# Keys by tokens through GpSimd, a transposing DMA and ScalarE instead of TensorE

## The reference

```python
Q = phi((xn @ Wq + bq)); K = phi((xn @ Wk + bk)); V = xn @ Wv + bv     # phi(z) = elu(z) + 1
def step(carry, qkv):                       # over the tokens
    KV = KV + einsum('bhd,bhe->bhde', ki, vi);  Ks = Ks + ki
    out = (qi . KV) / (qi . Ks + EPS)
y = x + out @ Wo + bo + tree(xn)
```

## Time and profile before

| | us |
|---|---|
| median of 3 runs | 1342.34 |
| lowest, highest | 1339.39, 1344.98 |
| the profiled execution | 1346.16 |
| its span in the profile | 1344.4 |

### The profile page before, as it was taken

The page is one execution under the profiler, slowest core; times in us unless marked ns, Lnnn a source line. Parts: engine busy times, 40 slices in busy tenths (PEclk is TensorE's granted clock), DMA queues, the critical chain, the costliest instruction groups (busy, mean ns, idle before and its releaser), DMA issues.

```text
span 1344.4 us, 49015 instructions
## 1 busy us (share of the span) xinstructions
PE 1266.5 (94%) x22173; PEld 1115.1 (83%) x22173; DVE 844.0 (63%) x2186; ACT 622.1 (46%) x1007; POOL 373.8 (28%) x590
## 2 busy tenths in 40 slices
PE   5899999999989999999999999999999999999987
PEld 4789788888978888888888888889788887887977
DVE  4775766657576574765757566574766757666463
ACT  3553544435445253553536445353553535545351
POOL 3424132141421413223141411413223141321410
PEclk9899999999999999999999999999999999999999
DMA  6000001000000000001000000100001000000000
GB/s 211 18 3 18 18 3 33 3 33 3 10 26 2 33 3 10 26 2 33 2 19 18 10 26 2 34 3 10 26 3 33 3 17 18 2 18 3 17 2 18
DMA packets 21599, 25.95 MB, mean 19 GB/s; under 512 B 1025, under 2 KB 19728, under 8 KB 21392
## 3 DMA queue, kind: packets, MB, share of 16 engines
q1 hardware_dynamic: 21392, 22.82, 5.2%
HBM read 14.43 MB, written 8.39 MB: 17 GB/s over the span
## 4 chain that ended last, share of the span: by engine, by line
PE 78%; DVE 11%; ACT 6%; issue 4%; DMA 1%; SPq 0%; DVEq 0%
PE w_pair L646 16%; PE s_pair L646 16%; PE o_pair L658 8%; PE s_pair L658 8%; PE kv_pair L727 5%; PE o_pair L752 5%; PE o_pair L766 5%; PE s_pair L716 4%; DVE xn L506 3%; PE w_pair L693 3%; PE w_pair L698 3%; ACT ex L407 3%; PE w_pair L680 3%; ACT ex L410 3%; DVE v_aug L529 2%
## 5 line engine op out<-in xcount | busy, mean ns | idle before, releaser
L329 POOL TENSOR_SCALAR_AFFINE_SELECT aT<-aT 64x512 f32<-64x512 f32 x256 | 167.6, 655 | 896.3 <-ACT aT L434 888.0
L646 PE MATMUL w_pair<-xnT,wk 128*128 128x512 f32 x768 | 209.5, 409 | 6.2 <-issue 3.6
L646 PE MATMUL s_pair<-xnT,wq 128*128 128x512 f32 x756 | 195.3, 394 | 0.2 <-issue 0.2
L434 ACT ACTIVATE aT<-s_pair 128x512 f32<-128x512 f32 x128 | 76.5, 597 | 251.6 <-PE s_pair L716 251.6
L577 DVE TENSOR_TENSOR snaps<-kv_pair,snaps 128x65 f32<-128x65 f32 x768 | 173.4, 226 | 26.4
L520 DVE SCALAR_TENSOR_TENSOR kT<-w_pair,bias_one,ex 128x512 f32<-128x512 f32 x128 | 95.9, 749 | 142.4 <-ACT ex L410 142.4
L646 PEld LDWEIGHTS s_pair<-xnT,wq 128*128 128x128 f32 x756 | 143.3, 190 | 32.0 <-issue 0.4
L646 PE MATMUL s_pair<-wv,xnT 128*128 128x512 f32 x648 | 168.6, 395 | 0.0
L646 PEld LDWEIGHTS w_pair<-xnT,wk 128*128 128x128 f32 x768 | 138.4, 192 | 33.1 <-issue 4.4
L410 ACT ACTIVATE ex<-ex 128x512 f32<-128x512 f32 x256 | 161.8, 632 | 8.1
L407 ACT ACTIVATE ex<-w_pair,neg_bias 128x512 f32<-128x512 f32 x130 | 89.4, 688 | 158.1 <-PE w_pair L646 158.1
(11 more groups left out here) (105 smaller groups left out, 2021.6 us busy)
## 6 DMA issues: line engine op xcount, KB each, us to landing
x_in<-in_L_attn_x_dram SPq DMA_DIRECT2D x16, 512.0 KB, 3.8
out_dram<-y_buf SPq DMA_DIRECT2D x32, 256.0 KB, 2.1
stage<-in_L_attn_Wv_dram SPq DMA_DIRECT2D x2, 512.0 KB, 8.1
stage<-in_L_attn_Wk_dram SPq DMA_DIRECT2D x2, 512.0 KB, 9.7
stage<-in_L_attn_Wq_dram SPq DMA_DIRECT2D x2, 512.0 KB, 10.8
stage<-in_L_attn_Wo_dram SPq DMA_DIRECT2D x2, 512.0 KB, 9.1
bv_all<-in_L_attn_bv_dram SPq DMA_DIRECT2D x1, 512.0 KB, 8.7
ffn_tok<-in_L_ffn_Wq_dram SPq DMA_DIRECT2D x1, 256.0 KB
```

Source lines behind the costliest of these rows:

```text
L329: pool.affine_select(out=part, in_=part, compare_op=ALU.is_ge, fill=0.0, base=0, pattern=[[0, 2 * CH], [1, D]], channel_multiplier=-1).the ...
L646: last = pe.matmul(dst, l, r, start=i == 0, stop=i == len(steps) - 1)
```

## The change

The first two units keep the old way. For every unit m from 2 on the keys by tokens are made without TensorE:

- GpSimd's `take_apart(m)` reads kT as 16-bit halves and lays the low halves of all 512 tokens in one plane and the high halves in another (k_planes). It waits until VectorE has made the keys, and until the DMA has read the planes of the unit before.
- SP's `turn_keys(m)` issues one transposing DMA, 128 x 1024 16-bit numbers, from k_planes to k_turned. It waits for GpSimd and until ScalarE is through with k_turned of unit m - 1.
- ScalarE's `put_together(m)` copies k_turned to k_tok and interleaves the halves again, one instruction of 128 x 1024 16-bit numbers. It stands behind the exponential of the queries.

So the fill "kT" leaves the list of a unit. The keys are now computed three units ahead, one more than before, and the queries stay two ahead. "oT" stands last before the "y" fills. TensorE waits for the new k_tok in the midst of the "oT" transposes. Some waits of TensorE are moved or split, `residual` goes from p = 0 to p = 1, the load of x from p = 0 to p = 2, and the stores of a block behind its last unit, on SP's queue. At p = 2 and p = 6 VectorE takes the value fills ahead of queries and output.

```diff
@@ unit_fills
-    ahead = divmod(n + 2, PAIRS) if n + 2 < blocks * PAIRS else None
+    keys = divmod(n + 3, PAIRS) if n + 3 < blocks * PAIRS else None
+    queries = divmod(n + 2, PAIRS) if n + 2 < blocks * PAIRS else None
...
+    fills.append((("oT", p, g), W1))
     if p == PAIRS - 1:
-        fills += [(("oT", p, g), W1), (("y", 0, g), O1)]
-    if ahead:
-        fills.append((("kT", ahead[1], ahead[0]), W0))
-    fills.append((("y", 1, g), S1) if p == PAIRS - 1 else (("oT", p, g), W1))
+        fills += [(("y", 0, g), O1), (("y", 1, g), S1)]
@@ FIRST
-         (("kT", 1, 0), W0)]
+         (("kT", 1, 0), W0), (("K", 2, 0), W0)]
@@ SP
+            def turn_keys(m):
+                sp.wait_ge(k_apart, m - 1)
+                if m > 2:
+                    sp.wait_ge(k_whole, m - 2)
+                sp.dma_start_transpose(k_turned[:, :, :], k_planes[:, :, :].rearrange("p s t -> p (s t)"))\
+                  .then_inc(k_turned_in, 16)
...
+            turn_keys(2)
+            for n in range(UNITS):
+                g, p = divmod(n, PAIRS)
+                if p == 0 and g:
+                    store(g - 1)
+                if n + 3 < UNITS:
+                    turn_keys(n + 3)
+                if p == 2 and g + 2 < BLOCKS:
+                    sp.wait_ge(x_consumed, g + 1)
+                    sp.dma_start(x_in[:, g % 2], x_rows[g + 2]).then_inc(x_loaded[g % 2], 16)
@@ GpSimd
+            def take_apart(m):
+                g, p = divmod(m, PAIRS)
+                pool.wait_ge(drained[bank_of["K", p, g]], count_of["K", p, g])
+                if m > 2:
+                    pool.wait_ge(k_turned_in, 16 * (m - 2))
+                pool.tensor_copy(k_planes[:, :, :], kT[:, m % 2].bitcast(U16).rearrange("p (t s) -> p s t", s=2))\
+                    .then_inc(k_apart, 1)
+                pool.wait_ge(k_apart, m - 1)
...
                     mask(n + 1)
-                if p == 0:
+                if n + 3 < UNITS:
+                    take_apart(n + 3)
+                if p == 1:
                     residual(g)
@@ ScalarE
+            def put_together(m):
+                act.wait_ge(k_turned_in, 16 * (m - 1))
+                act.wait_ge(kv_filled, m)
+                act.activation(k_tok[:, :, :].rearrange("p c f -> p (c f)").bitcast(U16)
+                               .rearrange("p (n s) -> p s n", s=2),
+                               k_turned[:, :, :].rearrange("p (s c) f -> p s (c f)", s=2), ACT.Copy).then_inc(k_whole, 1)
...
                     if kind in "KQ":
                         exponential(name)
+                        if kind == "Q":
+                            put_together(n + 2)
@@ VectorE
+            def values_first(fills, p):
+                if p not in (2, PAIRS - 2):
+                    return fills
+                return [f for f in fills if f[0] not in ("Q", "V0", "V1", "oT", "kT")] + \
+                    [f for f in fills if f[0] in ("V0", "V1")] + \
+                    [f for f in fills if f[0] in ("Q", "oT", "kT")]
@@ TensorE, the fill "oT"
                     for c in range(CH):
+                        if c == 1 and g * PAIRS + i + 1 < UNITS:
+                            until(a_masked, 2 * (g * PAIRS + i) + 4)
+                        if c == 2 and g * PAIRS + i + 2 < UNITS:
+                            until(k_whole, g * PAIRS + i + 1)
@@ TensorE, the outer products
-                until_drained(("kT", p, g))
+                if n < 2:
+                    until_drained(("kT", p, g))
+                else:
+                    until(k_whole, n - 1)
```

More of the change, by code:

```diff
@@ L46, in unit_fills @@
     fills = [(name, W1) for name in head]
-    if ahead:
-        fills += [(("K", ahead[1], ahead[0]), W0), (("Q", ahead[1], ahead[0]), S0)]
+    if keys:
+        fills.append((("K", keys[1], keys[0]), W0))
+    if queries:
+        fills.append((("Q", queries[1], queries[0]), S0))
     fills += [(name, S1) for name in tail]
+    fills.append((("oT", p, g), W1))
     if p == PAIRS - 1:
-        fills += [(("oT", p, g), W1), (("y", 0, g), O1)]
-    if ahead:
-        fills.append((("kT", ahead[1], ahead[0]), W0))
-    fills.append((("y", 1, g), S1) if p == PAIRS - 1 else (("oT", p, g), W1))
+        fills += [(("y", 0, g), O1), (("y", 1, g), S1)]
     return fills
@@ L282, in _, with store @@
             load("wo1")
[L284 to L287, removed]
+            def turn_keys(m):
[4 more added lines that the diff above has]
+                  .then_inc(k_turned_in, 16)
+            def store(g):
                 for i in range(2):
@@ L370, in _ @@
             pool.wait_ge(leaf_step, 1)
+            take_apart(2)
             for n in range(UNITS):
@@ L615, in _ @@
                     normalise(g + 1)
-                for name, _ in unit_fills(g, p, BLOCKS):
+                fills = [name for name, _ in unit_fills(g, p, BLOCKS)]
+                for name in values_first(fills, p):
                     kind, i, b = name
@@ L780, in scores_when_ready, with bank_free @@
                 g, p = divmod(n, PAIRS)
+                def bank_free(h):
+                    if n:
+                        until(drained[(S0, S1)[h]], uses_before[n - 1][(S0, S1)[h]])
+                    else:
+                        until_drained(("gate", h, 0))
                 if n:
-                    for bank in (S1, S0):
-                        until(drained[bank], uses_before[n - 1][bank])
                     until(s_copied, n)
-                else:
-                    for i in range(2):
-                        until_drained(("gate", i, 0))
                 until_drained(("Q", p, g))
-                scores(n)
+                scores(n, bank_free)
             def tiled(n):
@@ L867, in _ @@
                 tiled(n)
-                for name, bank in unit_fills(n // PAIRS, n % PAIRS, BLOCKS):
+                fills = unit_fills(n // PAIRS, n % PAIRS, BLOCKS)
+                first_by_vector = fills[0][0][0] in ("V1", "xT", "leaf")
+                for name, bank in fills:
                     kind, i, g = name
```

34 lines of the change are left out of this document (20 added, 14 removed).

## The result

| | median us | runs from to | profiled execution | its span | mean granted clock |
|---|---|---|---|---|---|
| before | 1340.9 | 1339.4 to 1345.0 | 1346.2 | 1344.4 | 0.991 |
| after | 1404.4 | 1404.0 to 1404.8 | 1404.0 | 1402.2 | 0.987 |

After takes 1.0464 times as long as before (95% interval 1.0440 to 1.0488): 63.5 us more. The forecast was 1418, the likeliest case's own range 1385 to 1450.

A forecast was written before the change was run, and what follows sets the result against it. TensorE, 94% busy, was taken to bound the kernel, with ScalarE's chain within 0.05 us of it. Median 1342.3 + 68 (units) + 12 (clock) - 4 (holes) = 1418 us; likeliest range 1385 to 1450, 8 in 10 from 1345 to 1500.

The forecast's parts named there:

- the likeliest case: Slower kernel, ScalarE's interleave holding up TensorE and the DMA hidden: 1418 us, range 1385 to 1450, chance 62%.
- The mechanism: Plain unit: TensorE waits 1.06 us at c == 2 for ScalarE's interleave behind the queries' exponential; unit 0.63 us longer.
- The sum over a block: Eight units of a block added up: 4.4 us longer, 66 us over 15 blocks, +68 us with the last block.
- The clock: Lower granted clock behind the hole at p = 7: 0 to 23 us lost, half taken, 12.
- The interleave: ScalarE's copy of 128x1024 16-bit numbers to k_tok: 1.05 us taken, bounds 0.6 and about 1.5.
- waits for keys and values: TensorE's 17 waits for keys (17 us) and 31 for last values (12 us with knock-on) go.
- holes ("issue"): TensorE's unexplained idle times may partly fall into the new waits: 0 to 19 us less, taken as 4.
- key transposes: Four transposes per unit leave TensorE in 126 of 128 units, 0.43 us each unit: 54 us less.
- rival 1: The transposing DMA doesn't land within a unit, from 7.25 us on: slower still, near 1500 or 1810 us; 20%.
- Rival 2: ScalarE's interleave is hidden, so the kernel is faster: 1259 us with no stall at all; 11%.
- Rival 3: No change: copy of 0.75 us, waits swallow the unexplained holes and the clock holds: 1346 us; 7%.
- GpSimd's copy: GpSimd's take_apart of 128x1024 16-bit numbers: 1.1 us taken, bounds 0.6 and 3, costing nothing.

The follow-up runs named there:

- side edits: Kernel before, keys still transposed on TensorE, with only values first on VectorE at p = 2 and 6 and the residual add at p = 1: 1311.1 us, ratio 0.978.
- the mask's wait: Kernel before with values first and the residual add moved, plus TensorE's wait for a_masked already at c == 1 of the output transposes: 1301.6 us, ratio 0.973.
- the doubled turn: Kernel after with the transposing DMA issued twice, the second after the first has landed: 1462.0 us, ratio 1.0905.
- the half copy: Kernel after with ScalarE's interleave replaced by a copy of 128x512 32-bit numbers from the untransposed keys, all waits kept: 1300.5 us, one run.
- flat copy: Kernel after with ScalarE's interleave replaced by a copy of 128x1024 16-bit numbers written one behind another, all waits kept: 1359.6 us, one run.

## Why the prediction was right, and where its numbers cancelled

**The mechanism.** Right in kind in each place: the wait at c == 2 is the one wait, in all 126 units. Predicted and measured in the plain unit: keys' relu at T+4.21, measured T+4.11; the hole 1.06, measured 1.08; the unit 8.38, measured 8.50. p = 3: 8.38 and 8.50. p = 0: 9.31 and 9.53. p = 7: a hole of 2.47 and 2.46. TensorE's busy share 86%, measured 87%.

**The sum over a block** was less right: +4.4 us without the clock, measured +3.5 (81.07 to some 84.6 with the clock kept). The plain units came out 0.12 us longer each, but p = 4, counted as a plain one, had already lasted 8.21 us before and grew by 0.28 instead of 0.63, and p = 7 grew by 0.26 (21.80 to 22.06 with the clock kept) instead of 1.64. The unit p = 7 that the prediction went by held an unexplained hole ahead of the keys' matmuls, and the sum carried it over into the kernel after, where it is gone:

```profile
520.81 1.10 PE L646 MATMUL w_pair<-xnT,wk 128*128 128x512 f32 x4 [1.29 <-issue]
```

**The clock** was luck in part. The mechanism stood on a row, but half of the 15 blocks was taken without a reason for half: 12 us. Measured are 8 blocks by 1.5 us, 12 as well.

**The interleave** was mis-sized: 1.05 us taken, 1.33 measured, inside the bounds of 0.6 to 1.5. Alone that is 126 x 0.28 = 35 us. Most of it did not reach the path: the relu came 0.10 us sooner after the start of the unit, and the interleave began 0.09 us before the recorded end of the exponential where I had put it 0.03 behind, 0.12 us sooner. 0.28 - 0.10 - 0.12 leaves 0.06, and the hand-over from c == 2 to the next unit took 0.37 instead of 0.31: together the 0.12 us by which the plain unit was too short.

**The credits** can be set against the runs one by one:

| us | predicted | measured | by |
|---|---|---|---|
| waits for keys and values (side edits) | -29 | -28 | 1338.6 to 1311.1 |
| holes ("issue") | -4 | -36 | 1311.1 to 1275.2, `o_normed` waits dropped |
| key transposes | -54 | -45 | 1275.2 to 1230.0 |
| the new stall, clock in it | +163 | +174 | 1230.0 to 1404.4 |
| sum | +76 | +65 | 1338.6 to 1404.4; +63.5 by the medians of the result |

The predicted +163 is the forecast's 76 with the three credits added back. The step that failed is the one on the holes: I let a few of them fall into the new waits, and they went altogether. Beside the old transposes it was the `o_normed` edit that took them away, one that I had passed over as having no price; no run puts those waits back into the kernel after. Against the forecast the stall came 11 us dearer, the holes gave 32 us more, the transposes 9 less, the side edits 1 less: 11 - 32 + 9 + 1 = -11 us of the 14 by which 1404 lies under 1418; the rest is the spread of the medians of before, 1338 to 1342. The sum was better than its terms. The measured column is a chain of runs, each less the one before, so that its sum is bound to come out: it is no test of the split. The split treats the edits as if their effects added up, and the mask's wait shows that not all do. Two bounds of the likeliest range don't follow from their own terms either (1342.3 + 68 - 20 is 1390, not 1391; 1342.3 + 68 + 23 + 13 is 1446, not 1449); nothing hangs on it.

**The rivals.** The turn (rival 1): 4 us taken, 3.2 measured in the median, 5.0 at the most. Of the two figures of the Trainium skill, that of the page "DMA: Bandwidth & Descriptors" (Latency and other measured facts; some 3 us, an estimate) agrees with 3.2, and the estimate made from "VectorE: DVE Perf Modes" (The three transpose paths; 10.5 us for eight blocks one behind another) does not. The threshold of 7.25 us was borne out by the doubled turn. Rival 2 (hidden): no copy of ScalarE was that fast, but its 1259 us understates what is there: with the interleave truly hidden, on GpSimd, it is 1230, mostly the missing credit for the holes. That credit also shifts its deciding point: with a copy of 0.61 us I had a plain unit still 0.18 us longer than before; with the half copy it is 0.03 longer (7.78 and 7.75), and that kernel takes 1300.5 us, less than before. Rival 3 (no change) wanted a copy of 0.75 us, which did not come. GpSimd's copy: 1.1 taken, 1.04 measured, hidden.

## What to carry to other kernels

Where work leaves the busiest engine, ask first on which engine its replacement lands and what stands ahead of it there: here the program with the interleave behind ScalarE's exponentials and the early wait is 174 us slower than the one with it on GpSimd and without that wait. Put a wait at the first instruction that needs the data; two transposes and 16 small matmuls too early cost 109 us. Before a step is moved earlier in an engine's order, follow its inputs around once: if they come from the step now behind it, a ring is closed and its length is the new unit.

## What the runs showed that I had not expected

- An activation over 128x1024 16-bit numbers takes 1.04 us written flat and 1.33 written interleaved; GpSimd's copy 1.04 us reading every other number, 1.36 writing so. 16-bit numbers were no faster than as many 32-bit ones.
- A transposing DMA of 128x1024 16-bit numbers occupied SP's queue for 1.23 us and landed after 3.1 to 5.0 us.
- Waits that are met long before they are reached can cost TensorE: dropping those for `o_normed` gave 36 us, most of it at other instructions than the waits.
- Holes of 2.46 us were followed by a lower granted clock in 8 of 15 blocks, those of 2.17 us (flat copy) in 3 of 15, those of 1.74 (half copy) in none, though in the kernel before one of 1.93 was followed by 0.59. So the length of the hole alone doesn't decide.
- A normalising instruction on VectorE that overlapped GpSimd's residual add ended 0.15 us after the add, in each of 15 blocks, and took 2.06 to 2.59 us; without the add beside it, it took 0.40.
